# Waits, orders and one group moved in the front stage of a graph and expert kernel

## The reference, cut to what matters

```
# layer 1, per graph: x = x + elu(gate * f_hom + (1 - gate) * f_het)
norm  = (sum(adj, -1) + 1e-6) ** -0.5
f_hom = (adj @ ((xn @ theta) * norm)) * norm          # xn = layernorm(x)
gate  = sigmoid(xn @ W_t + b_t);  f_het = xn @ W_h
# layer 2, per token: x = x + shared(xn) + routed(xn), 8 experts, top 2
shared = gelu(xn @ W1s + b1s) @ W2s + b2s             # 128 -> 512 -> 128
routed = sum over the two chosen experts of weight * expert(xn)
# layer 3: graph attention with 4 heads; layer 4: slices and a bidirectional scan
```

## Time and profile before

| | |
|---|---|
| median of 3 runs | 1468.7 us (1464.15 to 1470.95) |
| the profiled execution, its own time | 1468.55 us |
| its span in the profile | 1466.8 us |
| TensorE busy | 1370.2 us, 93% |
| VectorE, ScalarE, GpSimd busy | 969.2, 796.5, 583.3 us |
| front stage in the trace | 0 to about 671 us |
| loop over graphs | about 16 to 258 us |
| border and leading groups | about 258 to 336 us |
| routed groups, then trailing ones | to about 607 us, then to about 668 us |

### The profile page before, as it was taken

The page is one execution under the profiler, slowest core; times in us unless marked ns, Lnnn a source line. Parts: engine busy times, 40 slices in busy tenths (PEclk is TensorE's granted clock), DMA queues, the critical chain, the costliest instruction groups (busy, mean ns, idle before and its releaser), DMA issues. The chain is left out here.

```text
span 1466.8 us, 27059 instructions
## 1 busy us (share of the span) xinstructions
PE 1370.2 (93%) x9990; PEld 813.2 (55%) x9990; DVE 969.2 (66%) x2136; ACT 796.5 (54%) x1309; POOL 583.3 (40%) x502
## 2 busy tenths in 40 slices
PE   4999999899999999996899999999999789999998
PEld 1445555568999999862232232332333467774498
DVE  2466777543333333346889999999997799957633
ACT  2466564733444444433776776876764578873110
POOL 2026777672555555401021131132134598971000
PEclk9999999999999999998999999999999999999999
DMA  9846747355877777565434334233331321004034
GB/s 297 284 173 228 277 158 223 109 181 167 233 231 230 230 229 230 160 175 153 126 124 130 106 124 130 91 103 121 97 100 59 110 62 44 15 1 95 1 100 133
DMA packets 202391, 213.97 MB, mean 146 GB/s; under 512 B 22693, under 2 KB 159269, under 8 KB 202260
## 3 DMA queue, kind: packets, MB, share of 16 engines
q1 hardware_dynamic: 193620, 194.40, 43.5%
q0 software_dynamic: 8640, 17.84, 3.4%
HBM read 168.61 MB, written 43.58 MB: 145 GB/s over the span
## 5 line engine op out<-in xcount | busy, mean ns | idle before, releaser
L1445 ACT ACTIVATE c_AH<-c_S 128x2048 f32<-128x2048 f32 x128 | 240.7, 1880 | 138.7 <-PE c_S L1315 138.0
L1479 DVE TENSOR_TENSOR c_AH<-c_AH,c_A 128x2048 f32<-128x2048 f32 x128 | 292.1, 2287 | 26.5 <-ACT c_AH L1445 25.2
L829 ACT ACTIVATE a_A<-a_DG,a_A 128x256 f32<-128x256 f32 (+1 forms) x192 | 93.6, 526 | 206.7 <-PE a_DG L694 205.4
L589 POOL DMA_INDIRECT ys<-a_A,a_targets x142 | 137.8, 971 | 147.5 <-DVE a_A L1011 125.7
L565 POOL DMA_INDIRECT rows<-a_S,a_slots x128 | 133.8, 1046 | 50.4 <-issue 50.4
L1273 POOL TENSOR_TENSOR c_raw<-c_deg,c_power 128x16 f32<-128x16 f32 x16 | 53.8, 3361 | 246.5 <-DVE c_deg L1536 246.5
L1342 PE MATMUL c_DG<-c_AH,c_ones 128*32 128x512 f32 x1024 | 137.9, 611 | 4.9 <-DVE c_AH L1479 4.9
L1315 PE MATMUL c_S<-c_Q,c_K 32*128 32x512 f32 x928 | 132.3, 639 | 10.0 <-ACT c_AH L1445 6.5
L1328 PE MATMUL c_YA<-c_AH,c_XT 128*32 128x512 f32 x1024 | 131.9, 593 | 0.3 <-DVE c_XT L1546 0.3
L665 PE MATMUL a_AG<-a_A,x 128*128 128x512 f32 x256 | 114.1, 599 | 5.1 <-DVE a_Z L911 5.1
L694 PE MATMUL a_DG<-a_A 128*128 128x256 f32 (+1 forms) x336 | 99.9, 420 | 6.0 <-ACT a_A L829 6.0
(11 more groups left out here) (395 smaller groups left out, 2539.0 us busy)
## 6 DMA issues: line engine op xcount, KB each, us to landing
a_A<-in_dram SPq DMA_DIRECT2D x72, 578.0 KB, 5.0
a_A<-in_dram SPq DMA_DIRECT2D x32, 1024.0 KB, 9.5
c_A<-in_dram SPq DMA_DIRECT2D x128, 256.0 KB, 2.6
a_A<-rows SPq DMA_DIRECT2D x71, 130.0 KB, 3.5
a_X<-in_dram SPq DMA_DIRECT2D x8, 512.0 KB, 12.9
a_R<-in_dram SPq DMA_DIRECT2D x8, 512.0 KB, 4.8
stream<-a_R SPq DMA_DIRECT2D x8, 512.0 KB, 9.6
sums<-a_A SPq DMA_DIRECT2D x16, 256.0 KB, 2.5
```

Of the source, the lines that this page charges most:

```text
L589: pool.indirect_dma_start(ys, bass.IndirectOffsetOnAxis(ap=targets[g % NY][:, t:t + 1], axis=0), Y[g % NY][:, t, :], None, bounds_check=ys ...
L829: act.activation(hT[g % 2][:, f, 0:size(g)], up_bank(g, f)[:, 0:size(g)], ACT.Gelu, bias=w_of(g)[:, F_N + f:F_N + f + 1]).then_inc(h_ready, 1)
L1445: act.activation(AH[g % UNITS][:, :, :], S[:, :, :], ACT.Sigmoid, scale=HD ** -0.5).then_inc(att_ready, 1)
L1479: dve.tensor_tensor(ah[:, :, :], ah[:, :, :], A[g % ADJ_BUFS][:, :].unsqueeze(1).to_broadcast([P, HEADS, HALF]), ALU.mult).then_inc(ah_dve, 1)
```

## The change

It has five parts, all of them in the front stage but for one number.

1. `aggregate(i, 0)` waits for F tile by tile instead of for all 8 tiles. `aggregate(i, 1)` is cut after 4 matmuls, and `degree_transposes(i+1)` runs in the cut. VectorE reads the degrees before the statistics of graph `i+2`, and GpSimd computes the degrees' power before that of these statistics.
2. The border is reordered on all engines. ScalarE: a one-element Gelu ahead of `gelu(0)`, then `gelu(0)`, `gelu(1)`, and only then graph 7's exp, `share(6)`, `normalise_mid(6, 1)`, `gelu(2)`, `gelu(3)`, `normalise_mid(7, 0)`. TensorE: graph 7's `x2_transposes`, `logits` and `rank` go from between groups 2 and 3 to groups 4 and 5. VectorE: `finish` is cut in two at the wait for the exp, and `choose(6)` runs in between; `read_y(2)` stands before `choose(7)`, `read_y(3)` after it.
3. Ten leading groups instead of nine, so six trailing ones; graph 5 has 8 tiles to add in the attention stage instead of 4. The tenth group's input is loaded by `load_shared(9)` after the third store of y.
4. Graph 0's statistics come two groups later on VectorE, its norm one group later, and its transposes one group later on TensorE; the query and key matmuls go behind `down` of the last but one group.
5. On SP, the stores of y 1 and 2 and the tenth group's loads stand before the store of graph 7's `xT`, and the store of y 3 before `fill_ends`.

```diff
-LEADING = 9
+LEADING = 10
-TO_ADD = {1: T, 2: T, 3: T, 4: T, 5: T // 2}
+TO_ADD = {1: T, 2: T, 3: T, 4: T, 5: T}
...
 def load_shared(g):
-    if g >= 3:
-        sp.wait_ge(up_psum, FT * (g - 2))
+    before = max((p for p in range(g % 3, g, 3) if p not in left), default=None)
+    if before is not None:
+        sp.wait_ge(up_psum, FT * (before + 1))
...
             store_y(0)
+            store_y(1)
+            store_y(2)
+            load_shared(9)
             store_xT(B - 1)
-            store_y(1)
+            store_y(3)
             fill_ends()
-            store_y(2)
-            store_y(3)
             begin_routed()
...
+                if i + 1 < B:
+                    norm_power(i + 1)
                 if i + 2 < B:
                     n1.power(pool, power, i + 2, i % 2)
-                if i + 1 < B:
-                    norm_power(i + 1)
...
-            def aggregate(i, h):
-                pe.wait_ge(FZ_ready, T * i + T)
-                if i > 0:
+            def aggregate(i, h, part=range(T)):
+                if i > 0 and 0 in part:
                     pe.wait_ge(agg_ready, NH * (i - 1) + h + 1)
-                for t in range(T):
+                for t in part:
+                    if h == 0:
+                        pe.wait_ge(FZ_ready, T * i + t + 1)
                     mm = pe.matmul(...)
-                mm.then_inc(agg_psum, 1)
+                if T - 1 in part:
+                    mm.then_inc(agg_psum, 1)
...
-                aggregate(i, 1)
+                aggregate(i, 1, range(4))
+                if i + 1 < B:
+                    degree_transposes(i + 1)
+                aggregate(i, 1, range(4, T))
                 if i >= 2:
                     rank(i - 2)
-                if i + 1 < B:
-                    degree_transposes(i + 1)
...
             up(2)
-            x2_transposes(B - 1)
             down(1)
-            logits(B - 1)
             up(3)
-            rank(B - 1)
             down(2)
             for g in range(4, GROUPS):
                 up(g)
+                if g == 4:
+                    x2_transposes(B - 1)
+                if g == 5:
+                    rank(B - 1)
                 if is_routed(g + 1):
                     row_transposes(g + 1)
-                if g == GROUPS - 2:
+                if g == GROUPS - 1:
                     ... # transposes of x0
-                if g == GROUPS - 1:
-                    ... # query and key matmuls
                 down(g - 1)
+                if g == 4:
+                    logits(B - 1)
+            ... # query and key matmuls
             down(GROUPS - 1)
...
             copy_x2T(B - 2)
+            act.activation(warm[:, :], warm[:, :], ACT.Gelu)
             gelu(0)
+            gelu(1)
+            elu_exp(B - 1)
+            share(B - 2)
             normalise_mid(B - 2, 1)
-            elu_exp(B - 1)
-            gelu(1)
-            share(B - 2)
+            gelu(2)
+            gelu(3)
             normalise_mid(B - 1, 0)
-            gelu(2)
+            gelu(4)
             copy_x2T(B - 1)
             normalise_mid(B - 1, 1)
-            gelu(3)
-            share(B - 1)
-            for g in range(4, GROUPS):
+            for g in range(5, GROUPS):
                 gelu(g)
+                if g == 5:
+                    share(B - 1)
...
+            begin_finish(B - 1)
+            choose(B - 2)
             finish(B - 1)
-            choose(B - 2)
+            place(B - 2)
+            read_y(0)
             make_shift(n2, 1, B - 1, shift2)
-            read_y(0)
-            place(B - 2)
             read_y(1)
+            read_y(2)
             choose(B - 1)
+            read_y(3)
             place(B - 1)
             make_table()
-            read_y(2)
-            read_y(3)
...
-                if g == GROUPS - 5:
+                if g == GROUPS - 3:
                     ... # statistics of x0
-                if g == GROUPS - 3:
+                if g == GROUPS - 2:
                     ... # norm of x0 applied
-                if g == GROUPS - 2:
+                if g == GROUPS - 1:
                     ... # query and key read
```

More of the change, by code:

```diff
@@ L180, in front_stage @@
         Wg = sb("Wg", [P, E_N])
-        power = sb("power", [P, T])
+        power, warm = sb("power", [P, T]), sb("warm", [P, 1])
         keep = sb("keep", [P, E_N, T])
@@ L412, in load_shared @@
                 i, part = divmod(s, N // GS)
-                if g >= 3:
-                    sp.wait_ge(up_psum, FT * (g - 2))
+                before = max((p for p in range(g % 3, g, 3) if p not in left), default=None)
+                if before is not None:
+                    sp.wait_ge(up_psum, FT * (before + 1))
                 sp.wait_ge(xT_stored, 16 * (i + 1))
                 sp.dma_start(xT[g % 3], xT_all[i, :, bass.ts(part, GS)]).then_inc(xs_loaded[g % 3], 16)
-                if g >= 3:
-                    sp.wait_ge(y_read, g - 2)
+                if before is not None:
+                    sp.wait_ge(y_read, before + 1)
                 sp.wait_ge(mid_stored, 16 * (i + 1))
@@ L757, in _ @@
                         mm.then_inc(x0T_psum, 1)
-                if g == GROUPS - 1:
-                    pe.wait_ge(next_loaded, 48)
-                    pe.wait_ge(x0T_ready, NH)
-                    for k in range(2):
-                        pe.matmul(SIDE0[k], W3[:, k, :], xnT[:, half(0)], start=True, stop=True).then_inc(qk_psum, 1)
-                down(g - 1)
+                down(g - 1)
+                if g == 4:
+                    logits(B - 1)
+            pe.wait_ge(next_loaded, 48)
+            pe.wait_ge(x0T_ready, NH)
+            for k in range(2):
+                pe.matmul(SIDE0[k], W3[:, k, :], xnT[:, half(0)], start=True, stop=True).then_inc(qk_psum, 1)
             down(GROUPS - 1)
@@ L830, in gelu @@
                                    bias=w_of(g)[:, F_N + f:F_N + f + 1]).then_inc(h_ready, 1)
+            act.wait_ge(consts, 2)
+            act.activation(warm[:, :], ones[:, 0:1], ACT.Copy)
             normalise_in(0)
@@ L911, in read_transform, with begin_finish @@
                     dve.tensor_tensor(Z[i % 2][:, t, :], bank(t)[:, 2 * D:3 * D], bias[:, :], ALU.add).then_inc(FZ_ready, 1)
-            def finish(i):
+            def begin_finish(i):
                 u = i % 2
@@ L930, in finish @@
                                               op0=ALU.max, op1=ALU.add))
+            def finish(i):
+                u = i % 2
                 dve.wait_ge(E_ready, i + 1)
@@ L1043, in _ @@
                 if i >= 1:
+                    begin_finish(i - 1)
                     finish(i - 1)
@@ L1048, in _ @@
                     make_shift(n2, 1, i - 1, shift2)
+                if i + 1 < B:
+                    read_degrees(i + 1)
                 if i + 2 < B:
                     stats_in(i + 2)
-                if i + 1 < B:
-                    read_degrees(i + 1)
                 if i >= 2:
                     place(i - 2)
+            begin_finish(B - 1)
+            choose(B - 2)
             finish(B - 1)
-            choose(B - 2)
+            place(B - 2)
+            read_y(0)
             make_shift(n2, 1, B - 1, shift2)
-            read_y(0)
-            place(B - 2)
             read_y(1)
+            read_y(2)
             choose(B - 1)
+            read_y(3)
             place(B - 1)
             make_table()
-            read_y(2)
-            read_y(3)
             for g in range(4, GROUPS):
```

## The result

The kernel after takes 1457.93 us (median of 6 runs, 1455.29 to 1458.58) against 1468.79 for before on the same chip: ratio 0.9926, 95% interval 0.9911 to 0.9942. The forecast was 1458.9. The profiled execution took 1457.62 us, its span was 1455.9.

A forecast was written before the change was run, and what follows sets the result against it. TensorE, busy for 93% of the span, was taken as the bound, so only its stalls and low clock pay. Loop, border, tenth group, rows and graph 0 summed to -9.7 us: 1468.55 to 1458.9, range 1452 to 1464.

The forecast's parts named there:

- 8.8 predicted: Loop over graphs: removing TensorE's two waits gains 1.5 us, 1.0 us, then 0.80 + 0.72 - 0.26 in five graphs.
- the rank's stall: Loop: a new stall of 0.26 us ahead of `x2_transposes`, in the five graphs whose successor waits for a rank.
- the loop gains less: Rival: ScalarE or VectorE sets the loop's pace, which gains 4.2 instead of 8.8 us: 1463.5 us; chance 0.16.
- the exposed weight loads: Rival: the aggregation's waits expose TensorE's weight loads, 0.19 us for each of 56, 10.6 us: 1469.5; chance 0.05.
- predicted -1.0, -7.8, +2.8, +2.0: Border, in us: wait in `up(0)` shorter, stall and low clock at `up(1)` gone, new stall in `up(2)`, low clock behind.
- 3.8 forecast: First routed rows: TensorE stalls 3.8 us instead of 1.39, rows landing at 37.0 against a cover of 33.2.
- 1.3 forecast: Behind the wait for the first routed rows: 1.3 us lost to TensorE's low clock, bounds 0 and 3.1.
- the 3 to 5 us named as its sign: Sign at the first routed rows: a wait of 3 to 5 us ended by the DMA; under 2 or over 7 refutes.
- TensorE has nothing else to do there: First routed rows, in the rival that they come late and slow the kernel (chance 0.05): TensorE has no other work.
- +7.3 -7.0: Tenth leading group: adds 7.3 us ahead of the routed rows and saves 7.0 us among the trailing groups.
- forecast 1.9: Ahead of graph 0's transposes: the stall falls from 3.02 to 1.9 us, low clock behind it as before.
- +7.3 -7.0 -4.0 +3.7 -0.9: Forecast for parts 2 to 4, in us: tenth group added, trailing group saved, border, wait and clock at rows, graph 0.

The follow-up runs named there:

- rest_only: The kernel after with part 1 of the change taken back, so parts 2 to 5 alone: 1468.51 us, ratio 1.0007 to before.
- weights_first: The kernel after with all five routed weight loads issued ahead of the fills on SP: 1455.17 us, ratio 0.9906 to before.
- early_logits: The kernel after with graph 7's chain (norm, x2 transposes, logits, rank, place) put earlier: 1451.56 us, ratio 0.9873 to before.
- tile_waits_only: The kernel before with only part 1's tile-by-tile waits for F in the aggregation's first half: 1460.72 us, ratio 0.9938 to before.
- copy_for_exp: The kernel after with graph 7's exp done as a Copy, so its table loads go too: 1453.98 us, ratio 0.9907 to before.
- weights_late: The kernel after with one of five weight sets issued ahead of the first rows' loads, four behind: 1454.27 us, ratio 0.9902 to before.
- nine: The kernel after without its tenth leading group, so parts 1, 2, 4 and 5: 1462.18 us, ratio 0.9963 to before.
- eleven: The kernel after with eleven leading groups instead of ten: 1462.17 us, ratio 0.9965 to before.
- loop_x0: The kernel before with parts 1 and 4 of the change, nine leading groups and the old border: 1453.87 us, ratio 0.9893 to before.
- loop_only: The kernel before with part 1 of the change alone: 1456.68 us, ratio 0.9929 to before.
- early_first: The kernel after with graph 7's chain earlier, weights ahead of the fills, graph 0's norm directly behind its statistics: 1450.78 us, ratio 0.9878 to before.

## Why the prediction was right, and where it was off

**Part 1.** Right in mechanism, under-sized: 8.8 predicted. Of the 12.38 measured, 0.32 is an earlier start of graph 0. Another 1.74 is graph 0's transform, whose second half took 3.01 us instead of 4.75. That is the clock of one execution and no effect of the edit: behind the same wait of 1.88 or 1.89 us it took 3.01 in ten of the fourteen profiles here and 4.75 in four (before, rest_only, weights_first, early_logits). 10.3 are left: 1.60 in graph 0 and 1.63 in graph 1 (1.5 and 1.0 in the sum), 1.14 in graph 2, where TensorE stood 0.47 us ahead of the output's transposes, and 1.49 in each of the other four instead of 1.26. By the rows of before and after: 0.80 for the wait and 0.11 for the aggregation's first half, which the sum lacked; 0.76 for the degrees (0.72); and 0.18 for the rank's stall instead of 0.26, as the transposes behind it made up a part. In graphs 3 to 6 ScalarE was not late. tile_waits_only splits it into 0.91 and 0.58. The rival "the loop gains less" is refuted by the period, the exposed weight loads by the aggregation's 7.03 us for sixteen.

**Part 2.** Its TensorE terms were right: predicted -1.0, -7.8, +2.8, +2.0, and measured 0.96, the 4.72 gone, a wait of 2.59 and 1.47 of low clock. ScalarE's timeline ahead of that wait's end:

```profile
260.02 1.28 ACT L818 ACT_TABLE_LOAD   x1
261.31 1.06 ACT L818 ACTIVATE G<-G 128x1024 f32<-128x1024 f32 x1
...
265.56 1.28 ACT L836 ACT_TABLE_LOAD   x1
266.86 1.26 ACT L836 ACTIVATE a_A<-a_DG,a_A 128x512 f32<-128x512 f32 x2
```

By the Trainium skill, "ScalarE: Activation LUTs", "What ACT_TABLE_LOAD costs", the stall would have been 2.8 us longer, an estimate from its 2.66 us for a switch. The trace disagrees: the load at 265.56 takes 1.28 us and the gelu starts 1.30 us after the load's start, at 266.86. The same page of the Trainium skill, section "Table sets: the hidden batching unit", says to batch activations by table set. copy_for_exp agrees in direction: without the exp between the gelus the wait was gone. The kernel after also has a wait and a one-element Copy at ScalarE's start, to set the early Gelu's input, which the diff above leaves out; rest_only has them too, and its graph 0 starts at 25.20 against 25.25 in before.

**Parts 2 and 3 at the rows.** The term that was off in size is the wait, 3.8 forecast, 5.53 measured, and the low clock behind it, 1.3 forecast, 2.3 measured. The wait is outside the 3 to 5 us named as its sign, though not under 2 or over 7, which would have refuted the forecast. The cover was 33.5 us for 33.2 forecast (from logits' end at 291.59 to 325.09). The last scatter started at 321.06 - 291.59 = 29.5 instead of 28.1, the rows were asked for at 35.3 instead of 33.3 and used at 39.0 instead of 37.0. So the chain was 2.0 us long. 0.6 is the last scatter landing beside the weights. The other 1.4 isn't `place(7)`, whose scatters begin 8.5 us behind the logits for 8.7 forecast, but a gap in the scatters: the first at 300.09, the second at 302.93, with 1.87 us of idle ahead of it where 0.30 is the rule. weights_late shows that the weights hold some 4 us of the wait, early_logits that the chain holds 3.9 (5.53 to 1.61); the two overlap, and what neither removes is SP's order. The prediction said that TensorE has nothing else to do there. That is wrong: `down(8)` is independent of the rows and starts at 331.10, right behind their transposes. Ahead of them it might have hidden up to 3.6 us of the wait; no run tries it.

**Part 3.** Ten groups won some 5 us beside the new border (nine to after), but the forecast's balance (+7.3 -7.0, the cover bought at nothing) is the right way to say it: the group is only worth the wait that it hides. eleven shows the other end.

**Part 4.** Stall 1.65, forecast 1.9. The forecast kept a low clock behind the stall; there was none. In before it was 6.04 us from the first of graph 0's transposes to the next group's `up` (646.96 to 653.00), in after 4.50 (642.15 to 646.65). These 1.5 us, with a slightly shorter stall, make most of the 9.75 against 7.9. loop_x0 shows what the edit is worth where the trailing groups are seven: some 5 us, not 0.9.

**Unforeseen.** 2.0 us went at the start of the attention stage, from its first matmul to the transposes of x at 693.30 (704.40 in before), where VectorE waits for an adjacency tile. It goes with part 4: the wait was 2.17 to 3.23 us in all eleven kernels that have it and 0.45 to 1.31 in the three that don't (before, loop_only, tile_waits_only). loop_x0 and loop_only differ in part 4 alone: 2.17 against 0.45, and 34.1 against 33.0 us in this stretch. An earlier start of the stage is not the cause, since rest_only started it later than before (672.46 against 671.28) and waited 2.29. By what way part 4 delays the tile stays open.

**Balance.** The misses (loop 1.5 more, its 2.1 of chance, trailing 1.9 more, against border 1.0, rows' clock 1.0 and the attention stage 2.2) left 1.2 us between the forecast sum of -9.7 and the spans' -10.9. The figure was right partly by luck: errors of 1 to 2.2 us offset each other. By parts in ratios: part 1 -0.71%, part 4 -0.36%, part 2 (with 5) +0.70%, part 3 -0.37%, each good to about 0.25%, as the kernels compared ran in different groups. The sum of parts 2 to 4 in the forecast, +7.3 -7.0 -4.0 +3.7 -0.9, is -0.9 us, and rest_only says 1.0007 (-0.4 to +2.6 us): nothing won, as measured.

## What to carry to other kernels

When an edit removes stalls of the busiest engine at a hand-over, follow the chain that feeds the next stage from its first link: part 2 freed 5.1 us of TensorE and put that first link 9.4 us later. Put the chain's links at the earliest place where they fit, and buy cover with independent work only for what then remains; early_logits is some 8 us faster than after by that alone. Then look at which link waits last: once the scatters were early, it was a store that stands ahead of the loads on SP, and moving weights no longer helped. And split a diff before believing in its sum: here parts 1, 3 and 4 win, part 2 loses as much as 3 and 4 win together, and the net gain is the loop's. The two parts that need no new border, 1 and 4, are faster by themselves than the whole.

## What the runs showed of the hardware

- Behind one and the same wait TensorE came back at different clocks in different executions: after 1.88 or 1.89 us the second half of graph 0's transform took 3.01 us in ten profiles and 4.75 in four. After waits of 1.26 to 1.69 the work behind was at full clock in each row above. After 2.59 the next four matmuls took 1.98 in four profiles (nine, eleven, early_first, weights_late), 2.42 in early_logits and 3.45 in after; after 2.17 in tile_waits_only the `down` behind graph 0's transposes took 5.36 instead of 3.73. After the waits of 3.02 to 12.48 named here the work behind was slow each time (0.50 granted after 5.53 and 12.48). For a wait of 2 to 3 us the price was 0 to 1.6 us, and none of the rows shows what decides it.
- Five weight loads in flight went with 8.6 us from the last scatter's end to its row's use (after), one with 4.5 us (weights_late), and with the fills in the place of the weights it was 7.5 (weights_first). The Trainium skill, "Trainium Kernel Development and Optimization", "Key Constraints", says that the DMAs of all queues share 16 engines and interleave. The shares of 1.02 to 1.17 in these windows agree, and weights_first shows that swapping two bulk transfers on SP's queue moves the burden rather than lifting it.
- The scatter behind graph 7's first one came 1.87 us late instead of 0.30 in all seven kernels in which GpSimd had stood 1.4 to 5.7 us for graph 7's slots (after, nine, eleven, rest_only, copy_for_exp, weights_late, weights_first), though the program has no wait between the two. In early_logits GpSimd didn't stand there and it was on time; but in before it was on time too behind a stand of 2.71 us ahead of graph 6's scatters, so the standing alone does not explain it. I haven't traced its cause.
- The first half of an aggregation took 6.98 us with one wait in front of its sixteen records and 6.87 with a wait ahead of each tile. The second half took 6.96 to 6.97 in both kernels without idle time in front, so the 0.11 can't be put down to the wait as such.
